# The last sum of a convolution as an accumulating DMA of GpSimd, and the sum of x1 behind the choice of pairs

## The reference

```python
def block(x, ...):                       # x: (8, 1024, 128)
    h = _layernorm(_layernorm(x)) * gamma + beta
    h = _spiral_conv(h, ...)             # real part of a complex first-order recurrence along the sequence
    x1 = h + _layernorm(x)
    h = _layernorm(x1) * gamma + beta
    return silu(h @ w1 + b1) @ w2 + b2 + x1      # 128 -> 512 -> 128
x2 = x + block(x)
logits = einsum('th,eh->te', _layernorm(x2), router_w)   # 8 experts, the top 2, softmax over the two
return x2 + sum over the two experts of p_e * (gelu(xm @ w1_e + b1_e) @ w2_e + b2_e)   # 128 -> 256 -> 128
```

## Time and profile before

| | |
|---|---|
| median of 3 runs | 464.27 us (463.04 to 464.46) |
| span of the profiled execution, first to last instruction | 462.5 us; the median lies 1.8 us above it, and no other time of that execution is given |
| granted TensorE clock, mean | 0.934 |
| TensorE busy, matmuls | 379.4 us, 82% |
| VectorE busy | 357.4 us, 77% |
| ScalarE busy | 321.8 us, 70% |
| GpSimd busy | 268.1 us, 58% |
| chain that ended last, by engine | TensorE 56%, VectorE 16%, ScalarE 9%, GpSimd 4%, issue 5% |

### The profile page before, as it was taken

One profiled execution on the slowest core, in us unless ns is written; L12 is line 12 of the kernel. 1 busy time (PEld: TensorE's weight loads), 2 busy tenths in 40 slices (PEclk: granted clock), 3 DMA queues, 4 the chain that ended last, 5 costly groups with the idle time before them and its releaser, 6 DMA issues.

```text
span 462.5 us, 11382 instructions
## 1 busy us (share of the span) xinstructions
PE 379.4 (82%) x2812; PEld 339.3 (73%) x2812; DVE 357.4 (77%) x1329; ACT 321.8 (70%) x773; POOL 268.1 (58%) x331
## 2 busy tenths in 40 slices
PE   1274189989888889988897388999999999999980
PEld 1232168678676869686876388999999999999980
DVE  7999999978999999998176238777777777767770
ACT  4873387978887888867473536777777777777740
POOL 6980827452888888485627704676555555555551
PEclk9996569989999999999999569999999999999995
DMA  7649100000020202011203232444333333333200
GB/s 254 176 143 324 48 1 1 1 1 2 0 98 1 74 26 74 26 60 38 96 2 108 86 97 86 134 143 128 108 100 95 100 103 104 108 107 104 76 4 0
DMA packets 33283, 37.42 MB, mean 81 GB/s; under 512 B 5254, under 2 KB 29331, under 8 KB 33092
## 3 DMA queue, kind: packets, MB, share of 16 engines
q1 hardware_dynamic: 27236, 23.56, 18.0%
q0 software_dynamic: 5984, 13.13, 8.2%
HBM read 19.52 MB, written 18.92 MB: 83 GB/s over the span
## 4 chain that ended last, share of the span: by engine, by line
PE 56%; DVE 16%; ACT 9%; issue 5%; POOL 4%; POOLq 0%; DVEq 0%; ACTq 0%
PE up_p L999 12%; PE turn_p L999 6%; PE down_p L1018 6%; PE route_p L1018 6%; PE up_p L1018 5%; PE down_p L835 5%; PE turn_p L807 4%; DVE stats L1098 3%; ACT rows L655 3%; PE route_p L873 3%; ACT work L628 3%; PE down_p L1008 2%; DVE work L1162 2%; PE up_p L819 2%; DVE work L1160 1%
## 5 line engine op out<-in xcount | busy, mean ns | idle before, releaser
L590 POOL DMA_INDIRECT out<-result,out_id x91 | 89.2, 980 | 89.5 <-DVE result L1484 63.8
L556 POOL DMA_INDIRECT sorted_rows<-rows,pos x64 | 77.0, 1203 | 35.7 <-DVE pos L1217 18.4
L999 PE MATMUL up_p<-xt,work 128*128 128x128 f32 x488 | 66.5, 280 | 0.0
L781 ACT ACTIVATE work<-mw_c 128x256 f32 x182 | 65.5, 414 | 0.3 <-issue 0.2
L835 PEld LDWEIGHTS down_p<-w_sb,work 128*128 128x128 f32 x512 | 60.3, 192 | 4.9 <-issue 4.8
L835 PE MATMUL down_p<-w_sb,work 128*128 128x128 f32 x512 | 63.1, 277 | 0.0
L999 PEld LDWEIGHTS up_p<-xt,work 128*128 128x128 f32 x488 | 61.0, 196 | 0.2
L766 ACT ACTIVATE hid_t<-up_p 128x512 f32<-128x512 f32 x61 | 36.4, 597 | 30.3 <-PE up_p L999 29.7
L807 PE MATMUL turn_p<-ident,work 128*128 128x128 f32 x192 | 28.6, 298 | 28.4 <-ACT work L641 10.9
L615 ACT ACTIVATE work<-up_p,b_all 128x512 f32<-128x512 f32 x64 | 41.5, 680 | 14.3 <-PE up_p L821 14.2
L807 PEld LDWEIGHTS turn_p<-ident,work 128*128 128x128 f32 x192 | 24.0, 154 | 34.4 <-ACT work L641 11.6
(11 more groups left out here) (244 smaller groups left out, 896.5 us busy)
## 6 DMA issues: line engine op xcount, KB each, us to landing
tin<-sorted_rows SPq DMA_DIRECT2D x91, 136.0 KB, 2.1
resid<-in_x SPq DMA_DIRECT2D x8, 512.0 KB, 3.8
sorted_rows<-zeros SPq DMA_DIRECT2D x29, 136.0 KB, 2.3
out<-result,out_id POOLq DMA_INDIRECT x91, 2.2
work<-in_mw SPq DMA_DIRECT2D x1, 1024.0 KB, 6.2
sorted_rows<-rows,pos POOLq DMA_INDIRECT x64, 2.5
work<-in_w SPq DMA_DIRECT2D x1, 256.0 KB
w_sb<-in_w SPq DMA_DIRECT2D x1, 256.0 KB
```

The lines of the kernel that those rows point to most:

```text
L556: g.indirect_dma_start(sorted_dram, bass.IndirectOffsetOnAxis(pos[b % 2][:, j:j + 1], 0), rows[b % ROWBUFS][:, j, :], None).then_inc(s_sor ...
L590: g.indirect_dma_start(out_rows, bass.IndirectOffsetOnAxis(out_id[k][:, :], 0), result[k][:, :], None, bounds_check=TOKENS - 1, oob_is_err ...
L781: last = s_.activation(ring[s % RING][:, k * EF:(k + 1) * EF], mw1_c[:, bass.ds(at[k], EF)], ACT.Copy)
L999: last = t.matmul(mid_p[s % DEEP][:, c * TILE:(c + 1) * TILE], ring[s % RING][:, c * 128:(c + 1) * 128], xt[s % DEEP][:, :], start=True, s ...
```

## The change

1. VectorE's `convolution` is taken out everywhere. The subtraction becomes an addition: the table `out_im` is made with the opposite sign, and `in_re` and `in_im`, which are made from it, get theirs back (three table operations change an operand or a sign).
2. The two products signal a semaphore each (`s_tr`, `s_ti`), and GpSimd issues one accumulating DMA, SBUF to SBUF, 128 rows of 4 KB, `vi += vr`. It adds 16 to `s_conv` when it has landed, so `conv_turn` and the next `rotate_re` wait for 16 per batch. In GpSimd's queue it stands behind `sort_constants` (batch 0), behind `x0_scales(2)` (batch 1), and in iteration i, for batch i+2, behind tiles 0 to 3 of `sort_rows(i-2)` and ahead of tiles 4 to 7.
3. On VectorE, `x1_sum(i+1)` no longer follows `x2_sum(i-1)` at once; `x2_stats(i-1)` and `choose(i-2)` come between.

```diff
@@ -55,6 +55,7 @@
 ROWBUFS = 3
 INS = 8
 OUTS = 4
+BEFORE_CONV = 4
 
 DEEP = 3
 
@@ -130,7 +131,7 @@
         inv_abs = sb("inv_abs", [128, 1])
 
         start_v = sb("start_v", [128, 4])
-        neg_init_re = sb("neg_init_re", [128, 1])
+        neg_init_im = sb("neg_init_im", [128, 1])
         yk = sb("yk", [128, EXP_DEGREE])
         zz = sb("zz", [128, POWERS, 2])
         sq = sb("sq", [128, 4])
@@ -285,7 +286,8 @@
         s_u = sem("u_ready")
         s_ui = sem("u_im_ready")
         s_vi = sem("v_im_ready")
-        s_ti = sem("out_im_ready")
+        s_tr = sem("out_re_product_ready")
+        s_ti = sem("out_im_product_ready")
         s_conv = sem("conv_ready")
         s_t2 = sem("conv_turned")
         s_x1 = sem("x1_ready")
@@ -546,6 +548,12 @@
                 then(g.tensor_tensor(scale2[:, :], tmp[:, 7, :], neg_half[:, 0:TPB], ALU.pow))
                 g.tensor_tensor(shift2[:, :], tmp[:, 6, :], scale2[:, :], ALU.mult).then_inc(s_sc2, 1)
 
+            def convolution(b):
+
+                pool.wait_ge(s_tr, b + 1)
+                pool.wait_ge(s_ti, b + 1)
+                g.dma_start(vi, vr, accum_op=ALU.add).then_inc(s_conv, 16)
+
             def sort_rows(b, tiles):
 
                 if tiles[0] == 0:
@@ -566,14 +574,20 @@
                 if live(b3):
                     x0_scales(b3)
                 if live(chosen_b):
-                    sort_rows(chosen_b, range(TPB))
+                    sort_rows(chosen_b, range(BEFORE_CONV))
+                if live(b2):
+                    convolution(b2)
+                if live(chosen_b):
+                    sort_rows(chosen_b, range(BEFORE_CONV, TPB))
 
             decay()
             x0_scales(0)
             x0_scales(1)
             sort_constants()
+            convolution(0)
             x1_scales(0)
             x0_scales(2)
+            convolution(1)
             for i in range(LAST):
                 iteration(i)
 
@@ -837,7 +851,7 @@
                 last.then_inc(s_dn, 1)
 
             def conv_turn(b):
-                pe.wait_ge(s_conv, b + 1)
+                pe.wait_ge(s_conv, 16 * (b + 1))
                 if b == 0:
                     pe.wait_ge(s_u, 2)
                 after(pe, s_lo, b)
@@ -1145,7 +1159,7 @@
             def rotate_re(b):
 
                 v.wait_ge(s_u, b + 1)
-                after(v, s_conv, b)
+                after(v, s_conv, 16 * b)
                 return mark(d.tensor_tensor(vr, u, in_re, ALU.mult))
 
             def rotate_im(b):
@@ -1162,14 +1176,9 @@
                 d.tensor_tensor_scan(vi, decay, vi, start_v[:, 1:2], ALU.mult, ALU.add).then_inc(s_vi, 1)
                 if between:
                     between()
-                then(d.tensor_tensor(vr, vr, out_re, ALU.mult))
+                d.tensor_tensor(vr, vr, out_re, ALU.mult).then_inc(s_tr, 1)
                 v.wait_ge(s_vi, b + 1)
                 d.tensor_tensor(vi, vi, out_im, ALU.mult).then_inc(s_ti, 1)
-
-            def convolution(b):
-
-                v.wait_ge(s_ti, b + 1)
-                d.tensor_tensor(vi, vr, vi, ALU.subtract).then_inc(s_conv, 1)
 
             def low(b):
                 v.wait_ge(s_hi, b + 1)
@@ -1287,12 +1296,12 @@
                 b0, b1, b2, b4, chosen_b = i - 1, i + 1, i + 2, i + 4, i - 2
                 if live(b0):
                     x2_sum(b0)
-                if live(b1):
-                    x1_sum(b1)
                 if live(b0):
                     x2_stats(b0)
                 if live(chosen_b):
                     choose(chosen_b)
+                if live(b1):
+                    x1_sum(b1)
                 if live(b4):
                     counted = x_statistics(b4)
                 if live(b2):
@@ -1306,8 +1315,6 @@
                     scans(b2, rotated)
                 if live(b1):
                     low(b1)
-                if live(b2):
-                    convolution(b2)
 
             def weights():
 
@@ -1347,7 +1354,7 @@
                 re, im = low_high[:, 0, :, :], low_high[:, 1, :, :]
                 d.memset(re[:, :, 0:1], 1.0)
                 link(d.memset(im[:, :, 0:1], 0.0))
-                d.tensor_scalar(neg_init_re[:, :], par[:, INIT_RE:INIT_RE + 1], -1.0, None, ALU.mult)
+                d.tensor_scalar(neg_init_im[:, :], par[:, INIT_IM:INIT_IM + 1], -1.0, None, ALU.mult)
                 n, k = 1, 0
                 while n < STEP:
                     z_re = zz[:, k::POWERS // 2, 0:1].to_broadcast([128, 2, n])
@@ -1369,12 +1376,13 @@
                 d.tensor_tensor(out_re, out_re, vr, ALU.subtract).then_inc(s_ore, 1)
                 d.tensor_tensor(grid(out_im), slow[0], fast[1], ALU.mult)
                 link(d.tensor_tensor(grid(in_im), slow[1], fast[0], ALU.mult))
-                link(d.tensor_tensor(out_im, out_im, in_im, ALU.add))
+                link(d.scalar_tensor_tensor(out=out_im, in0=out_im, scalar=-1.0, in1=in_im, op0=ALU.mult,
+                                            op1=ALU.subtract))
 
                 v.wait_ge(s_ire, 1)
-                d.scalar_tensor_tensor(out=in_im, in0=out_im, scalar=neg_init_re[:, :], in1=vi,
+                d.scalar_tensor_tensor(out=in_im, in0=out_im, scalar=par[:, INIT_RE:INIT_RE + 1], in1=vi,
                                        op0=ALU.mult, op1=ALU.add)
-                d.scalar_tensor_tensor(out=in_re, in0=out_im, scalar=par[:, INIT_IM:INIT_IM + 1], in1=in_re,
+                d.scalar_tensor_tensor(out=in_re, in0=out_im, scalar=neg_init_im[:, :], in1=in_re,
                                        op0=ALU.mult, op1=ALU.add).then_inc(s_tab, 1)
 
 
@@ -1414,14 +1422,12 @@
             rotated = rotate_re(0)
             rotate_im(0)
             scans(0, rotated)
-            convolution(0)
             weights()
             x1_sum(0)
             x_moments(2, x_statistics(2))
             rotated = rotate_re(1)
             rotate_im(1)
             scans(1, rotated, lambda: low(0))
-            convolution(1)
             x_moments(3, x_statistics(3))
             iteration(0)
             for i in range(1, LAST):
```

## The result

| | before | after |
|---|---|---|
| median of the runs | 464.37 us (463.04 to 465.14, 4 runs) | **518.59 us** (517.39 to 519.64, 4 runs) |
| ratio to before, 95% interval | | 1.116 (1.1136 to 1.1184) |
| span of the profiled execution | 462.5 us | 517.3 us |
| mean granted clock of TensorE, share of full | 0.934 | 0.889 |
| start of `x2_sum` of batch 1 | 107.30 us | 119.52 us |

The change costs 54.2 us; the forecast was 45.0 (509.3), with a range of 496 to 531. The first `x2_sum` to be compared at full pace, that of batch 1, is 12.2 us late, and the five rounds behind it take 285.19 - 119.52 = 165.67 us in place of 123.31, 42.4 more. That makes 54.6 at `x2_sum(6)`; the rest of the kernel only starts later.

A forecast was written before the change was run, and what follows sets the result against it. The prediction took a closed loop of 24.07 us through all four engines, including x1_sum, as the bound. DMA start 14.9, order 28.4 and clock 1.7 made +45.0 on 464.27, so 509.3 us, range 496 to 531.

The forecast's parts named there:

- The bound of the kernel before: Batch rounds: a closed loop of 24.07 us round four engines, x1_sum on it because ScalarE normalises x1 before x2.
- Part 1: VectorE's order from iteration 2: x2 statistics and choice add 6.28 us to each of five rounds, +28.4 us.
- Part 2: VectorE's eight subtractions of about 1.2 us removed: hidden in its spare time but for once, 0.4 us taken.
- Part 3: Adding DMA of 6.6 us: uncovered in batches 0 to 2, +14.9 us; covered in batches 3 to 7.
- Part 4: TensorE's clock: falls before hn_turn cost slack alone, before x2's turn 1.7 us; one counted, round 6, +1.7 us.
- Rival 2: TensorE at half clock in every round: 516 us, chance 0.16.
- Rival 1: The DMA, over 7.5 us, sets the loop in the rounds: 522 us at 9.0, 543 at 12; chance 0.22.
- Rivals 3 to 5: Light DMA, 496 to 499.5 us (0.06); VectorE the bound, 454.7 (0.03); change does nothing, 464 (0.02).
- the forecast's own bounds: Whole kernel with a DMA of 3.8 to 7.5 us and a loop of 30.35: 500 to 512 us, chance 0.51.

The follow-up runs named there:

- e1: Kernel before with only VectorE's order changed, x1_sum behind x2_stats and the choice; VectorE still subtracts, no adding DMA: 507.74 us, ratio 1.0934.
- e5: Kernel before with only x2_stats put ahead of x1_sum, the choice staying behind it: 483.04 us, ratio 1.0405.
- e9: Kernel before with x2_stats ahead of x1_sum, and x2 handled ahead of x1 on GpSimd and ScalarE too: 461.95 us, ratio 0.9946.
- e10: Changed kernel with x2 ahead of x1 on GpSimd and ScalarE, VectorE's order left as it is: 497.02 us, ratio 1.0689.
- e2: Changed kernel with x1_sum second in VectorE's order again, leaving the accumulating DMA alone: 496.05 us, ratio 1.0702.
- e6: Changed kernel with VectorE adding for batches 0 to 2 and the DMA only from batch 3 on: 511.63 us, ratio 1.1032.
- e4: e1 with VectorE's rotation made to wait for GpSimd's scales of x1 and x2: 507.06 us, ratio 1.0943.
- e7: e1 with unread filler matmuls on TensorE, 14 ahead of hn_turn and 10 ahead of xm_turn: 506.29 us, ratio 1.0918.
- e3: Changed kernel with unread filler matmuls on TensorE ahead of hn_turn and xm_turn: 526.69 us, ratio 1.1351.
- e11: e9 with the adding DMA making the sum from batch 3 on: 480.69 us, ratio 1.0351.
- e8: e1 with the edits of both e4 and e7: 501.17 us, ratio 1.0796.

## Why the prediction was right, and where it fell short

- **The bound of the kernel before: right.** The sum of x1 stood on the closed loop, because x1 is normalised ahead of x2. e1 shows it (+43.5 us for an order), and e5 against e9 shows the reason: the same delay of `x1_sum` goes with +18.8 us when x1 is normalised first, and with -2.3 when x2 is. For the whole delay this is shown only beside the DMA (e10), not without it.
- **Part 1, the order: right in its 6.28 us**, 6.43 in the profile. The step "All of it is inserted in the closed loop: 24.07 + 6.28 = 30.35 us" was too narrow, since it treated the loop of before as the only one. The delay of `x1_sum` lengthens a second path, through `hn_turn`, by as much. The sum also charges the order from iteration 2 on only. In iteration 1 the statistics of x2 already stand ahead of `x1_sum(2)`, and without any DMA `x2_sum(1)` is 4.2 us late in e1.
- **Part 2, the subtraction: as forecast in the profile.** VectorE is idle for 3.08 us ahead of each `x2_sum` and 6.41 ahead of the positions, so the subtraction was hidden. No run takes it out by itself.
- **Part 3, the DMA: right mechanism, somewhat too dear.** I took 6.6 us. From the end of the products (40.95, 65.99, 88.12) to the turn's start it was 6.2, 5.3 and 5.2 us, and the median from issue to landing is 4.8. The start costs 12.2 us at `x2_sum(1)`, 14.9 forecast for the DMA alone; e2, the DMA without the order, has 11.5 there, and e6 says that 8.8 of the 12.2 go with the DMA. The two causes overlap. The row of 1024 KB, by its bytes read, was the wrong neighbour; that of 512 KB and 1 us more would have done. The cover held in the rounds in that `x1_sum` was never released by the DMA's turn there. It was not free: TensorE waited 2.66, 0.22, 2.27 and 2.28 us for the landing at the head of rounds 3 to 6, and e1 without the DMA has 2.4 us less in its five rounds. That the landing came within 2.7 us of `x2_sum`, and not 5.4 behind it, is also owed to rounds 2 to 4 us longer than forecast. The estimate of 4.4 us from the Trainium skill ("Collectives: The Full Stack", Part 3, with the fit in "DMA: Bandwidth & Descriptors", Anatomy of one DMA) came nearer to the landing's 4.8 than I did. Used as I used my 6.6, from the products to the turn, it is 0.8 to 1.8 us short, and my figure 0.4 to 1.4 long.
- **Part 4, the clock: this step failed.** "TensorE will now stand idle before `hn_turn` (held back by `x1_sum`) for several us, where a fall costs slack alone". It costs more. The fall makes the second path the longer one, and `x2_norm` comes 2.8 us late in the round shown. And "where it costs 1.7": a fall ahead of `xm_turn` cost 2.45 and 2.81 us, and there were two, not one. (The 1.7 also sets a start of the timeline, 93.72, against one of the chain, 194.65; with 194.54 of the timeline it is 1.6.) The account of the rounds: 42.36 measured, 30.1 forecast (28.4 and 1.7); all five are longer than the 30 to 32 us it named. Of the 12.2 us between, 3.6 are the dearer falls ahead of `xm_turn` (5.3 less 1.7), 7.9 are `x2_norm` coming late in rounds 2 to 5, and 0.7 is 18.51 + 11.99 = 30.50 instead of 30.35 a round.
- **What of the 7.9 us is whose** follows only in part. In round 3 the chain runs through GpSimd's shift of x1, which takes 1.61 us instead of 0.20: that is its 1.4. In rounds 2, 4 and 5 it runs through TensorE at half clock; e4 shows that the stretched shift is hidden behind that path, and rounds 2 and 5 of e7 that GpSimd's stretched scales take its place where the clock holds. Of rounds 2, 4 and 5 the clock is thus the cause, but some 1.0 to 1.4 us of it a round would have been paid to the shift anyway. In e3, the changed kernel with the clock at 1.00 behind `hn_turn` in rounds 2 and 4, these rounds are only 0.7 us shorter each, and scales of x1 are stretched in both (a shift of 1.63 us at 134.43, two steps of 1.26 and 1.15 from 200.68). The division is worked out from single profiles; no run prices the clock by itself.
- **The rivals.** Rival 2, half clock in every round, at 516, came nearest in time: a turn at half clock stands in every round of the table. It was wrong on the place and the price alike. Its argument against itself, that one fall makes TensorE late and so closes the next gap, fits the rows: rounds with a slow `hn_turn` have an `xm_turn` at full speed. Rival 1 did not happen in the changed kernel, but does in e2 and e11. Rivals 3 to 5 fell.

In sum the under-estimate of 9 us is 12.2 too little in the rounds and 2.7 too much at the start. 518.6 lies above the forecast's own bounds of 500 to 512; the range holds it because it reached up over rivals 1 and 2, and neither is what happened. That the time fell into the range is in part luck; what the prediction had right is the order's cost through the loop.

## What to carry to other kernels

Before you move work off the engine that looks full, find what the loop passes through, and ask which of two results the *next* engine takes first: here a delay of `x1_sum` by 2.2 us a round went with 18.8 us more (e5), or with 2.3 us less when ScalarE and GpSimd took x2 first (e9). When a wait is lengthened, every branch that hangs on it gets longer, also those that had slack; check the second longest one with TensorE at half clock, since the wait itself can bring that about. Matmuls put into the gap are no sure cure: they cost 8 us in e3 and gained 1.5 in e7. And an asynchronous operation that takes four times as long as the instruction it replaces needs a round with that much slack between its inputs and its reader, the first rounds included.

## What the runs showed of the hardware

**An adding DMA of 512 KB from SBUF to SBUF, issued by GpSimd,** lands 4.8 us after its issue (4.6 to 5.5 over eight), against 3.8 for a plain load of the same size from DRAM, issued by SyncE, and takes 0.9 to 1.1 us of GpSimd.

**GpSimd's small operations wait for VectorE's two-input ones.** The shift of x1, eight values a partition, takes 0.20 us alone (265.30, in round 6 of the changed kernel). Beside VectorE's second product of the rotation (from 199.87, for 1.22 us, above) it takes 1.15 and ends with it:

```profile
198.26 1.67 POOL L540 TENSOR_TENSOR scale<-tmp,neg_half 128x8 f32<-128x8 f32 x1
200.00 1.15 POOL L541 TENSOR_TENSOR shift<-tmp,scale 128x8 f32<-128x8 f32 x1
```

With the rotation held back, in e4, the same instruction:

```profile
186.33 0.20 POOL L539 TENSOR_TENSOR shift<-tmp,scale 128x8 f32<-128x8 f32 x1
```

In e7 one that starts at 223.95 takes 1.95 us and ends at 225.90, together with VectorE's first scan (223.56 + 2.34). The Trainium skill, "SBUF — State Buffer", section "SBUF: two separate sides", says that the two engines share a pair of ports under an exclusive lock, and that a VectorE operation with two inputs in SBUF takes it against GpSimd's reads for the whole instruction. By that rule a small operation would end with VectorE's, not run slower in proportion; the trace agrees, both ends falling within 0.1 us of each other.

**TensorE's clock**, told by the time of the turn behind the gap, fell to 1.2 GHz behind idle times of 2.81, 3.82, 4.57, 4.91, 5.33 and 7.02 us in the changed kernel from 93 us on, and stayed at 2.4 GHz behind 1.63 to 1.74, 2.27, 2.28, 2.46, 2.66 and also 3.29. The profile's clock agrees: it is 1.00 for the 4 us from the gap of 3.29 (93.30 to 97.30), and 0.50 from the one of 4.57 (175.30 to 179.00). The turn alone can mislead: in e8 it takes 1.09 us behind 2.03, 2.06 and 1.96, and the clock falls right behind or late in it (0.53 from 152.20 to 155.80), while in e7 it is 1.00 for the 5.7 us behind a gap of 2.06 (118.50 to 124.20). The length of the gap alone does not decide; what else does stays open here.
